# Rows of the experts in fixed regions of DRAM, and tokens routed by groups of four tiles

## The reference

```
x = x + 0.5 * moe8(layernorm(x))                      # top-1 of 8 experts, 128 -> 512 -> 128, relu
x = x + windowed_attention(layernorm(x))              # 16 heads of 8, window of 32
x = x + 0.5 * moe8(layernorm(x))
x = x + 0.5 * latent_block(layernorm(x))              # causal attention over 2048 tokens, then top-1 of 4 experts
x = x + state_space(layernorm(x))                     # a long convolution
x = x + 0.5 * latent_block(layernorm(x))

moe(x): logits = x @ gate_w.T + gate_b; e = argmax(logits)
        y = relu(x @ W1[e].T + b1[e]) @ W2[e].T + b2[e]
```

## Time and profile before

| | us |
|---|---|
| median of 3 runs | 1850.19 |
| lowest, highest | 1843.22, 1853.05 |
| the profiled execution | 1851.78 |
| its span | 1850.5 |
| PE busy | 1266.9 |
| DVE busy | 1233.6 |
| ACT busy | 930.3 |
| POOL busy | 502.0 |

### The profile page before, as it was taken

How to read it: one execution, slowest core, us unless ns; L and a number is a source line. 1 busy time by engine, 2 the same in 40 slices (tenths; PEclk the granted TensorE clock), 3 DMA queues, 4 the chain that set the end, 5 groups by cost and what they waited for, 6 DMA issues and landing times. The chain is left out here.

```text
span 1850.5 us, 41738 instructions
## 1 busy us (share of the span) xinstructions
PE 1266.9 (68%) x16199; PEld 658.5 (36%) x16199; DVE 1233.6 (67%) x3276; ACT 930.3 (50%) x1457; POOL 502.0 (27%) x956
## 2 busy tenths in 40 slices
PE   2755555437466778889888373755678789988736
PEld 2743444427453212222223263434222222222336
DVE  4358688743656799998774245156788999877325
ACT  0216522202334568978888132034357588878602
POOL 2321122223445341132012333034433100111233
PEclk9977555558756899999999587756589999999858
DMA  8710000002100000000000081000000000000012
GB/s 238 147 42 1 25 5 5 3 26 61 43 1 2 1 1 1 1 2 3 2 1 2 26 230 34 2 1 1 1 1 1 1 2 1 2 2 2 7 52 72
DMA packets 63618, 48.53 MB, mean 26 GB/s; under 512 B 6544, under 2 KB 58624, under 8 KB 63072
## 3 DMA queue, kind: packets, MB, share of 16 engines
q1 hardware_dynamic: 57744, 35.02, 7.6%
q0 software_dynamic: 4736, 9.74, 1.7%
q10 hardware_dynamic: 944, 1.10, 0.2%
HBM read 28.36 MB, written 16.46 MB: 24 GB/s over the span
## 5 line engine op out<-in xcount | busy, mean ns | idle before, releaser
L1437 ACT ACTIVATE arena<-psum 128x1024 f32<-128x1024 f32 (+3 forms) x640 | 559.9, 898 | 179.0 <-PE psum L1347 167.8
L1482 DVE TENSOR_REDUCE arena<-psum 128x1 f32<-128x512 f32 x768 | 479.8, 683 | 68.2 <-PE psum L1337 64.4
L1363 PE MATMUL psum<-arena 128*9 128x256 f32 (+2 forms) x4352 | 343.2, 392 | 2.3 <-POOL arena L1536 2.2
L1337 PE MATMUL psum<-arena 64*128 64x512 bf16 (+3 forms) x1280 | 241.4, 373 | 118.8 <-DVE arena L1482 57.9
L1487 DVE CUSTOM_DVE_ANT_0 arena<-psum,wqkv 128x384 bf16<-128x384 f32 (+3 forms) x512 | 230.2, 486 | 75.2 <-PE psum L1337 73.9
L1347 PE MATMUL psum<-arena 64*128 64x512 bf16 (+3 forms) x1280 | 231.5, 359 | 11.3 <-ACT arena L1437 5.5
L1337 PEld LDWEIGHTS psum<-arena 64*128 64x128 bf16 x1280 | 64.0, 94 | 374.5 <-DVE arena L1482 199.4
L1536 POOL TENSOR_SCALAR_AFFINE_SELECT arena<-arena 128x256 f32<-128x256 f32 x256 | 103.7, 408 | 323.0 <-ACT arena L1437 320.5
L1363 PEld LDWEIGHTS psum<-arena 128*9 128x9 f32 x4352 | 67.4, 89 | 174.5 <-issue 134.0
L518 DVE TENSOR_SCALAR small<-psum,YT 128x128 f32<-128x128 f32 x168 | 50.5, 342 | 106.3 <-PE psum L438 105.5
L1514 POOL CAST arena<-arena 128x16 bf16<-128x16 f32 x64 | 16.4, 257 | 330.3 <-DVE arena L1493 328.1
(11 more groups left out here) (272 smaller groups left out, 1932.3 us busy)
## 6 DMA issues: line engine op xcount, KB each, us to landing
arena<-taps SPq DMA_DIRECT2D x8, 1024.0 KB
ACCn<-sorted_rows SPq DMA_DIRECT2D x16, 258.0 KB, 3.6
big_w<-in_w SPq DMA_DIRECT2D x2, 2048.0 KB, 20.2
ACCn<-made_rows SPq DMA_DIRECT2D x16, 256.0 KB, 3.9
sorted_rows<-arena SPq DMA_DIRECT2D x2, 1483.5 KB, 14.6
sorted_rows<-arena SPq DMA_DIRECT2D x2, 1225.5 KB
w<-in_w SPq DMA_DIRECT2D x2, 1024.0 KB
X<-in_L_attn_x SPq DMA_DIRECT2D x4, 256.0 KB, 4.8
```

What stands on the lines that cost most here:

```text
L1337: pe.matmul(psum[:, b, 0:w], plain_q[v % 2][rows, a, i * P:(i + 1) * P], keys[rows, 2 * hq + a, c * GW:c * GW + w], start=True, stop=True) ...
L1363: mm = pe.matmul(psum[32 * hh:32 * hh + 9, O_BANK, lo:hi], values[:, tile_of(v, j), 4 * hq + hh, :], prob[(t + hh // 2) % N_PROB][:, hh % ...
L1437: act.activation(prob[t % N_PROB][:, :, off:GW], both, ACT.Exp, scale=INV_SQRT_HD).then_inc(a_got, 1)
L1482: dve.tensor_reduce(place, bank[:, 0:w], AX.X, ALU.max).then_inc(a_max_got, 1)
```

## The change

- DRAM has a tensor `regions` in which expert e has the rows from 2048 e on, shared by the stages c = 1 to 3. A token's slot is the start of its expert's region plus the number of earlier tokens of that expert, so a group of tiles can be given its slots when the groups before it have theirs (`pick_dve`, `place_pe`, `slots_dve`; `seen` keeps the counts so far). It can be scattered at once (`scatter_pool`).
- When all groups are done, `count_pe` and `tables_dve` (22 instructions on DVE) work out each sorted tile's expert, its first row in the regions and which of its rows hold tokens. `moe_sp` reads that row number into a register and issues one DMA for each tile. The target row of an output is no longer in the row itself: `set_index` puts it together with the rows that hold no token.
- The three later blanks go. In their place `fill_regions_sp` copies the blank of the first stage, which that stage's scatter has by then partly overwritten, over all of the regions, on SP after the first MoE's `made_back_sp`.
- c = 0 keeps its global sort. c = 1 is routed in `normed_and_routed`, group by group inside the layer norm, with all its scatters on POOL.
- In the latent blocks groups 3, 2 and 1 are normed, routed and scattered by events of the list beside the last units (`mean`, `root`, `norm`, `turn`, `logits`, `pick`, `place`, `slots`); group 0 comes after the list. `project` and `square` of groups 1 and 0 come earlier than before.

In the new list the tail reads, with places: `project` 1 at 648.8, `square` 1 at 650.8, `take` 14 at 652.8, `mean` and `root` at 653.0, `norm` 655.0, `out` 14 at 656.8, `turn` 3 at 657.0, `logits` 3 at 659.0, `cut` (15, 2, 1) at 660.4, `place` 3 at 661.0, `slots` 3 at 661.1, `cut` (15, 3, 0) at 662.4, `slots` 2 at 663.1, `cut` (15, 3, 1) at 664.4, `slots` 1 at 665.1, the last `weigh` of unit 15 at 667.6, `take` 15, `out` 15. Before, `project` 1 was at 652.8 and `square` 1 at 660.8.

```diff
-        sorted_rows = [nc.dram_tensor(f"sorted_rows{c}", (SLOTS, D + 1), F32).ap() for c in range(4)]
+
+        sorted_rows = nc.dram_tensor("sorted_rows", (SLOTS, D + 1), F32).ap()
+        regions = nc.dram_tensor("regions", (NE0 * T + SLOTS, D + 1), F32).ap()
...
-        def blank_rows(c):
-            slots = sorted_rows[c].rearrange("(s p) d -> p s d", p=P)[:, 0:TILES[c], :]
-            sp.dma_start(slots, blank[:, 0:TILES[c], :]).then_inc(blanked[c], 16)
...
+        def pick_dve(c, k, logits, gate_b, order, read=None):
+
+            n_exp = EXPERTS[c]
+            of_i = lambda v: v.rearrange("p (i e) -> p i e", e=n_exp)
+            log, eq = (of_i(small[:, j, 0:GT * n_exp]) for j in range(2))
+            hot = of_i(small[:, 2, k * GT * n_exp:(k + 1) * GT * n_exp])
+            best, best2 = small[:, 3, 0:GT], small[:, 3, 8:8 + GT]
+            done(dve.tensor_tensor(log, of_i(logits), gate_b[:].unsqueeze(1).broadcast_to([P, GT, n_exp]), ALU.add), read)
+            chain(dve.tensor_reduce(best, log, AX.X, ALU.max))
+            chain(dve.tensor_tensor(eq, log, bcast(best, n_exp), ALU.is_ge))
+            chain(dve.tensor_tensor(eq, eq, order[:].unsqueeze(1).broadcast_to([P, GT, n_exp]), ALU.mult))
+            chain(dve.tensor_reduce(best2, eq, AX.X, ALU.max))
+            dve.tensor_tensor(hot, eq, bcast(best2, n_exp), ALU.is_equal).then_inc(hot_made, 1)
+            dve.wait_ge(hot_made, slots_done(c, k))
...
+        def place_pe(c, k, to):
+
+            n_exp = EXPERTS[c]
+            hot = small[:, 2, k * GT * n_exp:(k + 1) * GT * n_exp]
+            pe.wait_ge(hot_made, slots_done(c, k))
+            pe.matmul(to, above[:], hot, start=True, stop=False)
+            for i in range(GT - 1):
+                one = hot[:, i * n_exp:(i + 1) * n_exp].unsqueeze(1).broadcast_to([P, GT - 1 - i, n_exp])
+                mm = pe.matmul(to[:, (i + 1) * n_exp:GT * n_exp].rearrange("p (i e) -> p i e", e=n_exp), ones[:], one, start=False,
+                               stop=(not k and i == GT - 2))
+            if k:
+                pe.wait_ge(seen_made, NG * (c - 1) + k)
+                mm = pe.matmul(to.rearrange("p (i e) -> p i e", e=n_exp), ones[:],
+                               seen[:, 0:n_exp].unsqueeze(1).broadcast_to([P, GT, n_exp]), start=False, stop=True)
+            return mm
...
+        def slots_dve(c, g, k, places, read=None):
+            n_exp = EXPERTS[c]
+            of_i = lambda v: v.rearrange("p (i e) -> p i e", e=n_exp)
+            place, hot = of_i(small[:, 4, 0:GT * n_exp]), of_i(small[:, 2, k * GT * n_exp:(k + 1) * GT * n_exp])
+            to, more_seen = small[:, 3, 16:16 + GT], small[:, 3, 32:32 + n_exp]
+            done(dve.tensor_tensor(place, of_i(places), region_start[:, 0:n_exp].unsqueeze(1).broadcast_to([P, GT, n_exp]), ALU.add), read)
+            chain(dve.tensor_tensor(place, place, hot, ALU.mult))
+            chain(dve.tensor_reduce(to, place, AX.X, ALU.add))
+            dve.tensor_copy(slot[:, rows_of(g)], to).then_inc(slots_made, 1)
+            by_expert = hot.rearrange("p i e -> p e i")
+            if k == 0:
+                dve.tensor_reduce(seen[:, 0:n_exp], by_expert, AX.X, ALU.add).then_inc(seen_made, 1)
+            else:
+                chain(dve.tensor_reduce(more_seen, by_expert, AX.X, ALU.add))
+                dve.tensor_tensor(seen[:, 0:n_exp], seen[:, 0:n_exp], more_seen, ALU.add).then_inc(seen_made, 1)
+            dve.wait_ge(seen_made, NG * (c - 1) + k + 1)
...
+        def count_pe(c):
+            pe.wait_ge(seen_made, NG * c)
+            pe.matmul(psum[:, 4, 0:EXPERTS[c]], ones[:], seen[:, 0:EXPERTS[c]], start=True, stop=True).then_inc(counted, 1)
...
+                    for s in chunk(c, q):
+                        row = sp.value_load(tile_row[0:1, s:s + 1], min_val=0, max_val=(EXPERTS[c] - 1) * T + s * P)
+                        sp.dma_start(rows_of_tiles(s, s + 1)[:, 0, :], regions[bass.ds(row, P), :]).then_inc(tile_in[q], 16)
+
+        def fill_regions_sp():
+
+            filled = 0
+            while filled < NE0 * T + SLOTS:
+                n = min(SLOTS, NE0 * T + SLOTS - filled)
+                sp.dma_start(regions[filled:filled + n, :], sorted_rows[0:n, :]).then_inc(regions_in, 16)
+                filled += n
...
+        def scatter_pool(c, g, k, rows, to):
+            pool.wait_ge(slots_made, slots_done(c, k))
+            for i in group(g):
+                pool.indirect_dma_start(to, bass.IndirectOffsetOnAxis(slot[:, i:i + 1], 0), rows[:, i, :], None).then_inc(rows_out, 16)
...
+            def set_index(q):
+
+                lo, hi = chunk(c, q)[0], chunk(c, q)[-1] + 1
+                dve.wait_ge(tile_in[q], tiles_in(c, q))
+                dve.copy_predicated(index[:, lo:hi], valid[:, lo:hi],
+                                    number_in(rows_of_tiles(lo, hi))[:, :, 0]).then_inc(index_set, 1)
...
+                pool.wait_ge(blanked, 16)
+                for g in range(NG):
+                    scatter_pool(c, g, g, Yn, sorted_rows)
...
+            if c == 0:
+                fill_regions_sp()
...
+            for g in range(NG + 3):
+                if 1 <= g <= NG:
+                    ln_rows(n, g - 1)
+                if g < NG:
+                    x_ready(g)
+                    ln_statistics(n, g)
+                    ln_rooted(n, g)
+                if 1 <= g <= NG:
+                    copy_turned(f, g - 1)
+                if g >= 3:
+                    dve.wait_ge(place_made, NG * (c - 1) + g - 2)
+                    slots_dve(c, g - 3, g - 3, psum[:, 4, 0:W_])
+                if 2 <= g < NG + 2:
+                    dve.wait_ge(logits_made, NG * c + g - 1)
+                    pick_dve(c, g - 2, psum[:, g - 2, 0:W_], gateb0, order0)
+            tables_dve(c)
+            pool.wait_ge(regions_in, REGIONS_IN)
+            for g in range(NG):
+                scatter_pool(c, g, g, Yn, regions)
...
+        ROUTED = sorted(LAST, key=lambda g: LAST[g])
...
-                    places += [(after[6 + 4 * k] - 0.2, name, ORDER[v][0]) for k, name in enumerate(("rows", "project", "square"))]
+                    steps = (6, 10, 14) if ORDER[v][0] in ROUTED[:2] else (6, 8, 9)
+                    places += [(after[k] - 0.2, name, ORDER[v][0]) for k, name in zip(steps, ("rows", "project", "square"))]
+                if v == LAST[ROUTED[-2]]:
+                    places += [(after[10], "mean", 0), (after[10] + 0.1, "root", 0), (after[11], "norm", 0)]
+                    for k, g in enumerate(ROUTED[:-1]):
+                        places += [(after[12 + k], "turn", g), (after[13 + k], "logits", g), (after[13 + k] + 0.1, "pick", g),
+                                   (after[14 + k], "place", g), (after[14 + k] + 0.1, "slots", g)]
...
+                    elif kind == "root":
+                        act.wait_ge(o_mean, 2 * B + 1)
+                        act.activation(rstd[:, GT:NT], rstd[:, GT:NT], ACT.Sqrt).then_inc(o_root, 1)
...
+                    elif kind == "mean":
+                        dve.wait_ge(o_squared, NT * B + NT - GT)
+                        dve.tensor_scalar(rstd[:, GT:NT], rstd[:, GT:NT], 1.0 / D, EPS_RMS, ALU.mult, ALU.add).then_inc(o_mean, 1)
+                    elif kind == "norm":
+                        dve.wait_ge(o_root, 2 * B + 1)
+                        chain(dve.reciprocal(rstd[:, GT:NT], rstd[:, GT:NT]))
+                        for g in ROUTED[:-1]:
+                            scaled_rows(g)
...
                             times_c(2 * x - 13)
+                    elif kind == "slots":
+                        scatter_pool(c, x, ROUTED.index(x), ACCn, regions)
...
+            g, k = ROUTED[-1], NG - 1
             dve.wait_ge(o_squared, NT * (B + 1))
-            dve.tensor_scalar(rstd[:, :], rstd[:, :], 1.0 / D, EPS_RMS, ALU.mult, ALU.add).then_inc(o_mean, 1)
-            act.wait_ge(o_mean, B + 1)
-            act.activation(rstd[:, :], rstd[:, :], ACT.Sqrt).then_inc(o_root, 1)
-            dve.wait_ge(o_root, B + 1)
-            chain(dve.reciprocal(rstd[:, :], rstd[:, :]))
-            for i in range(NT):
-                dve.tensor_scalar(ACC[:, i, :], Y[:, i, :], rstd[:, i:i + 1], None, ALU.mult).then_inc(o_rows, 1)
-            dve.tensor_copy(number_in(ACCn), token_number.unsqueeze(2)).then_inc(dve_step.sem, dve_step.up())
-            dve.wait_ge(dve_step.sem, dve_step.n)
-            turn_rows_pe(f, ACC, o_rows, NT * B, gate1, NE1)
-            turn_rows_act(f, norm_w[:, 1:2])
-            route_dve(c, gateb1, order1)
-            route_pe(c)
+            dve.tensor_scalar(rstd[:, rows_of(g)], rstd[:, rows_of(g)], 1.0 / D, EPS_RMS, ALU.mult, ALU.add).then_inc(o_mean, 1)
+            act.wait_ge(o_mean, 2 * B + 2)
+            act.activation(rstd[:, rows_of(g)], rstd[:, rows_of(g)], ACT.Sqrt).then_inc(o_root, 1)
+            dve.wait_ge(o_root, 2 * B + 2)
+            chain(dve.reciprocal(rstd[:, rows_of(g)], rstd[:, rows_of(g)]))
+            scaled_rows(g)
...
```

(13 more changed lines are left out.)

200 lines of the change are left out of this document (152 added, 48 removed).

## The result

The changed kernel takes 1873.23 us, the kernel before 1849.03 us, medians of four runs each that took turns on one chip. The ratio is 1.0128 with an interval of [1.0095, 1.0161]: slower by some 24 us. The profiled execution after took 1868.55 us, the lowest of its runs; its span is 1867.3, against 1850.5 in the earlier trace rows.

The account below looks back on a forecast made before the run. No engine is busy over 68%, so borders between stages, where POOL scatters alone, matter. Fill +53.6, second routing -10, latent blocks -2: +41.6 us, median 1892 us, 2.3% slower; range 1858 to 1913, the forecast's own 1880 to 1903.

Parts of the forecast that it names:

- Term 1: Windowed attention after the first MoE: the 9.97 MB fill on SP's queue delays the bias loads, uncovered, by 53.6 us.
- half of 381 is 190, which falls back on 53 us: Fill's rate: each byte crosses DRAM twice, so even the fastest loads' 381 GB/s halves, giving 53 us again.
- The lower end, 26.2 us: Shortest fill time considered, at 381 GB/s, the trace's fastest window, of big contiguous loads.
- The row of the blanks: Profile row for blanks writing 516 B rows to DRAM from SP's queue: 186 GB/s, taken as the fill's rate.
- the upper end of 66: Longest fill time considered, 66 us, at the 151 GB/s the blanks moved without the scatters beside them.
- rival 1: Fill after the first MoE is fast, 26.2 us, its pieces contiguous: 1864 us, DVE starting at 145; chance 0.17.
- Rival 3: At the windowed attention, SP's queue lets the bias loads past the fill: -12 to -32, about 1835 us; chance 0.11.
- Rival 2: Latent blocks' tails hide the routing, POOL taking its cuts in time: -11 us twice, fill full, 1872 us; chance 0.10.
- What the fill replaces: Three blanks of 4.45 MB under the first MoE: removing them gives nothing, as PE was busy beside them.
- Term 2: Second routing (macaron, 8 experts): scatters start inside the layer norm, -14.5 us, tile loads +4.5; -10 us, from -13 to -7.
- Term 3: Two latent blocks, routing beside the last unit: later output +19.0, then -9.2, scatters -15.3, first tiles +4.5; -1.0 us each.
- The drop of the clock: Latent blocks' thin stretch: PE falling to its lower clock would double its matmuls there, about +3 us.

## Why the prediction was right, and what it mis-sized

The sign was right, and so was the mechanism of the largest term. The time lies in the range, 1858 to 1913, which was made wide enough for the rivals; it doesn't lie in the forecast's own, 1880 to 1903. The likeliest time was 1892, 19 us too high at the median.

**Term 1, right in its mechanism, 24 us too large.** The biases are held by the fill, nothing covers it, and moving it behind them gives 28.3 of the 29.8 us back. The rate was mis-sized. The step that failed is "half of 381 is 190, which falls back on 53 us": that a byte crosses DRAM twice doesn't halve the rate, for the fill moved 334 GB/s, close to the 381 of the loads in the earlier trace rows. The lower end, 26.2 us, was worked out from that row and was 3.6 us off. The row of the blanks was nearest by operation and by row size, but the fill isn't made of pieces of 516 B: both its sides are contiguous, and it went in 208 packets of 48 KB. In pieces of 516 B, spread over DRAM as the blanks were, it takes 77.6 us, beyond the upper end of 66. So the pieces decide, by a factor of 2.6 (their length, or with it their order, which was changed too). The direction counts for less: 334 against 381 GB/s in long pieces, 128 against 151 or 186 in short ones. DVE's start at 151.0 lies by the sign given for rival 1 (145), and not by the forecast's (172).

The Trainium skill's 207 to 214 GB/s for copies between DRAM tensors (page "DMA: Bandwidth & Descriptors", section "Latency and other measured facts") would have made it 47 us. Its copies had rows of 16 KiB, each 512 KiB or more behind the last; the trace has 334 GB/s for pieces of 48 KB that lie one behind the other, and here the measurement decides.

Rival 3, that the queue lets the biases past, fell; with the fill on ACT or POOL the queues do take turns, and the biases still come no sooner. Rival 1 had nearly the right size of the fill: its 1864 us are 9 us below the median, the forecast's 1892 are 19 above. Rival 2's 1872 us are the nearest number, and that by chance: it has the fill at 53.6 us and the latent blocks at -11 each, and they were 29.8, +2.0 and +2.75.

**What the fill replaces** was put at nothing. Without the blanks beside it the first MoE is from its first tile to its first read back 53.3 us instead of 54.6, so 1.4 us, inside what one execution differs from another.

**Term 2, right in sum, less so in its parts.** The first scatter starts 13.9 us behind the norm (forecast 14.7), the last one ends 35.5 behind it (forecast 35.0), and the first tile comes 4.0 us later behind it than before (forecast 4.5). But POOL was not the bound throughout: it waited for the slots of the third group (1.29 us) and the fourth (0.68), so that 21.6 us lie between the first scatter and the end of the last, and not 20.3. The sum counted DVE's instructions and left out that DVE stands still for 2.5 us at each of these groups, until PE has its places; the last group's slots are done 30.8 us behind the norm, where 26.8 was forecast. The tables are 19 instructions and not 22, and they end at 437.7, 0.8 us behind the last scatter, where they were to lie under it. A tile costs SP 1.09 us, where 1.26 was worked out from DVE's copies. The misses nearly cancel.

**Term 3, -1 forecast, +2.0 and +2.75 measured.** By its own steps in the first block:
- The root is done 11.6 us behind unit 13's output, as forecast (1016 behind 1004.4).
- Unit 15's output comes +21.2 us later behind unit 13's, forecast +19.0. The scatters of the three groups and the cuts stood in POOL's order as foretold, and the last cut ended at 1054.89. But the sum followed POOL alone; PE's queue with the picks ends at the same time, as the experiment with the scatters behind the cuts showed. So rival 2 couldn't have come true by POOL taking its cuts in time. From the root to the first slot numbers it is 9.9 us, forecast 8.6: transposes, copy and logits of the first group stand in PE's queue behind weighing that the lower clock makes longer (1.90 us for eight matmuls of 512 columns at 0.50, against 1.05 before at 1.00). A place of the later groups is 2.4 us of PE from the last pick on (1051.48 to 1053.92), where 1.5 was taken: it is five matmuls and not four, since the counts of the earlier groups are added by one more, and it stands at the lower clock. The drop of the clock was told as an end of the range, not in the sum.
- From there to the first scatter it is 7.0 us shorter, forecast 9.2: transposes, copy and logits of the one group take 3.9 us (1067.2 to 1071.1) where 2.4 was taken, and the place 2.5 where 1.9 was.
- The scatters give 15.4 us, forecast 15.3, and the first tiles cost 3.1, forecast 4.5.

Together 21.2 - 7.0 - 15.4 + 3.1 = +1.9. The step that failed is the size of the thin stretch: the short steps of one group on PE, which were priced too low and in part at the wrong clock. How much of it is the clock alone, no run separates.

**Overlooked.** The wait for `order` ahead of the first layer norm was in the diff and in no term: +1.9 us, which go when it is taken away.

## What to carry to other kernels

A large transfer that nobody waits for yet belongs behind the small loads that somebody waits for, in the order of issue of all engines and not only of its own queue: here that order was the whole difference between a change that loses 1.3% and one that loses nothing. Another queue doesn't help: where queues take turns by the packet, the one with short packets gets next to no bytes beside the one with long ones. To price a transfer, look first at how long its contiguous pieces are, then at its direction.

Work that is moved beside the end of another stage is free only where every queue it passes has room, PE's too; when one group's routing already hides behind another's scatters, moving it earlier has little left to give.

## What the runs showed of the hardware

- DRAM to DRAM, from SP's queue: 334 GB/s in packets of 48 KB, 128 GB/s in packets of 516 B that lie 128 rows apart. Writes of rows of 516 B from SBUF were at 186, with scatters beside them.
- Two queues with work move the same number of packets (96 and 96 in 10 us, 98 and 98 with the fill on POOL), whatever their length: 3.09 MB of the fill against 0.05 MB of SP's. 1 MB of reads back then takes 35.1 or 32.4 us to land, against 3.3.
- The issue of a load of 64 KB on SP is held for 26.4 to 28.6 us while 10 MB issued from ACT or POOL and the 1 MB of reads back in its own queue are under way.
- A DMA whose DRAM address comes from a register that SP reads from SBUF costs SP 1.09 us, against 0.51 for one with a fixed address.
